# A decoder layer with rotary attention and a gated Hadamard FFN: queries and keys rotated feature-major and stored as score-ready rows, four attention units' maxima taken beside the FFN, division by the softmax sums moved to the output

## The reference, cut to what matters

```python
x  = L0_attn_X                                  # (4, 1024, 256)
xn = _layernorm(x)                              # over the 256 features
# attention, 16 heads of 16
Q, K, V = xn @ Wq.T, xn @ Wk.T, xn @ Wv.T
r0 = cos * x0 - sin * x1                        # x0, x1: even and odd features of a head
r1 = sin * x0 + cos * x1
scores  = einsum('bhqd,bhkd->bhqk', Qr, Kr) * 16 ** -0.5
scores  = where(causal, finfo.min, scores)
pattern = softmax(scores, axis=-1)
s = einsum('bhqk,bhkd->bqhd', pattern, V) @ Wo.T
# FFN
h = fwht(xn * SU_ug) / 64
h = silu(h @ W_gate.T * ws_gate * 64) * (h @ W_up.T * ws_up * 64)
g = silu(fwht(h * SU_dp) / 64 @ W_down.T * Wscale_dp * 64)
out = x + s * g
```

## Time and profile before

| what | before |
|---|---|
| median of 3 runs | 1056.6 us (1055.76 to 1058.85) |
| profiled execution, its own time | 1058.22 us |
| its span | 1056.5 us |
| TensorE (PE) busy | 944.7 us, 89% |
| VectorE (DVE) busy | 702.3 us, 66% |
| ScalarE (ACT) busy | 489.1 us, 46% |
| GpSimd (POOL) busy | 196.1 us, 19% |
| TensorE clock granted, mean | 0.962 of full |

### The profile page before, as it was taken

One profiled execution on the slowest core, in us unless ns is written; L12 is line 12 of the kernel. 1 busy time (PEld: TensorE's weight loads), 2 busy tenths in 40 slices (PEclk: granted clock), 3 DMA queues, 4 the chain that ended last, 5 costly groups with the idle time before them and its releaser, 6 DMA issues. The chain is left out here.

```text
span 1056.5 us, 17971 instructions
## 1 busy us (share of the span) xinstructions
PE 944.7 (89%) x6560; PEld 600.6 (57%) x6560; DVE 702.3 (66%) x1274; ACT 489.1 (46%) x729; POOL 196.1 (19%) x359
## 2 busy tenths in 40 slices
PE   5699999999999978889888888888888888888887
PEld 1488888888888865444444544444444444445355
DVE  6756465564655647677778778777877777787325
ACT  2332333333332320366565656656565665556641
POOL 4200000000000100122222222232222223221226
PEclk9899999999999995599999999999999999999989
DMA  5102112022030220011101201210210212012124
GB/s 177 41 1 100 67 33 99 0 99 93 6 129 14 86 83 37 5 73 42 63 19 42 76 11 37 82 37 7 81 37 14 74 42 76 7 41 87 51 70 180
DMA packets 46982, 61.19 MB, mean 58 GB/s; under 512 B 19008, under 2 KB 30272, under 8 KB 46912
## 3 DMA queue, kind: packets, MB, share of 16 engines
q1 hardware_dynamic: 45296, 57.11, 16.2%
q10 hardware_dynamic: 1616, 3.15, 1.0%
HBM read 34.81 MB, written 25.17 MB: 57 GB/s over the span
## 5 line engine op out<-in xcount | busy, mean ns | idle before, releaser
L926 DVE TENSOR_REDUCE maxes<-ps 128x1 f32<-128x512 f32 (+3 forms) x640 | 372.1, 632 | 75.1 <-PE ps L775 62.3
L885 ACT ACTIVATE probs<-ps 128x1024 f32<-128x1024 f32 (+3 forms) x384 | 296.7, 809 | 173.6 <-PE ps L796 169.8
L767 PE MATMUL ps<-k_t,q_t 64*128 64x512 f32 (+3 forms) x768 | 223.5, 406 | 51.1 <-DVE maxes L926 50.9
L767 PEld LDWEIGHTS ps<-k_t,q_t 64*128 64x128 f32 x768 | 116.6, 195 | 118.9 <-DVE maxes L926 108.2
L717 POOL TENSOR_SCALAR_AFFINE_SELECT probs<-probs 128x256 f32<-128x256 f32 x256 | 104.6, 409 | 398.5 <-ACT probs L885 396.1
L796 PE MATMUL ps<-q_t,k_t 64*128 64x512 f32 (+3 forms) x768 | 164.8, 418 | 3.5 <-ACT probs L885 2.2
L811 PE MATMUL ps<-probs,v_ones 128*32 128x512 f32 (+3 forms) x1536 | 165.7, 504 | 0.2 <-POOL probs L717 0.2
L796 PEld LDWEIGHTS ps<-q_t,k_t 64*128 64x128 f32 x768 | 77.1, 188 | 90.0 <-ACT probs L885 54.3
L242 PE MATMUL ps<-xh,wug_hi 128*128 128x512 f32 x256 | 101.4, 396 | 2.6 <-DVEq L336 2.6
L314 ACT ACTIVATE silu<-ps,scales 128x512 f32<-128x512 f32 x64 | 44.1, 689 | 126.9 <-PE ps L242 126.9
L367 DVE SCALAR_TENSOR_TENSOR hid<-ps,scales,silu 128x512 f32<-128x512 f32 x64 | 48.1, 751 | 82.1 <-ACT silu L314 82.1
(11 more groups left out here) (94 smaller groups left out, 1151.4 us busy)
## 6 DMA issues: line engine op xcount, KB each, us to landing
loaded<-scr_qkv SPq DMA_DIRECT2D x16, 768.0 KB, 4.3
scr_qkv<-qkv SPq DMA_DIRECT2D x8, 1152.0 KB, 4.4
x_sb<-in_x SPq DMA_DIRECT2D x10, 512.0 KB, 4.6
scr_gate<-y_sb SPq DMA_DIRECT2D x8, 512.0 KB, 3.9
gate_in<-scr_gate SPq DMA_DIRECT2D x8, 512.0 KB, 5.4
xt_in<-in_xt SPq DMA_DIRECT2D x8, 512.0 KB, 6.3
scr_heads<-o_nat SPq DMA_DIRECT2D x32, 128.0 KB, 2.3
out_t<-res SPq DMA_DIRECT2D x8, 512.0 KB, 2.7
```

Of the source, the lines that this page charges most:

```text
L767: last = pe.matmul(ps[:, bank, n * w:(n + 1) * w], q_t[par][rows, p, i * P:(i + 1) * P], k_t[par][rows, p, part * CH:part * CH + w], start ...
L885: act.activation(probs[:, (NS * par + s) % RING, p, :, 0:w], ps[:, bank:bank + 2, 0:w], ACT.Exp, scale=SCALE).then_inc(exp_ok, 1)
L926: dve.tensor_reduce(maxes[:, part, i, 2 * pairs[0] + e:2 * pairs[-1] + e + 1:2], ps[:, turns['m', k, e], 0:n * w].rearrange('p (h k) -> p ...
```

## The change

Projection block. The q and k projections are made feature-major (weights stationary, 512 tokens streaming; even and odd features of all heads in two banks), rotated by four wide VectorE products a chunk (turn) and added by GpSimd, split by ScalarE and GpSimd, and stored by SyncE in twelve transfers a chunk as rows that can be loaded as score operands (store_kinds): 48 rows for each head, high, high, low for queries and high, low, high for keys. hid_lo and the next chunk's normalisation move from VectorE to GpSimd. The chunk is 24 slots with a ring of four banks. From chunk 2 on, the 80 max tiles of units 2, 3, 0, 1 (in this order) and their 8 row transposes are spread over the slots, with two banks of their own. The loops over chunks are written out.

Attention block. No slots, to_rows, to_tokens, split_hi, split_lo or copies; operands come by DMA straight from scr['qk'], 48 of 64 rows of each half used (49 with the row of maxima). The 240 tiles of units 4 to 15 are spread over steps 3 to 174 of 192: 68 steps hold two, 104 one, 20 none. Each unit's rows are loaded twice, for the tiles (q_m, k_m) and for the scores (q_s, k_s). The undivided products go to HBM. A chain of steps (CHAIN) for each of 6 chunks then loads the sums, inverts them, writes the inverses to HBM, reads them back spread over the heads' rows, multiplies on GpSimd, and makes the output products among the steps (piece). Chunks 6 and 7 stay behind the last step. The output block is gone.

```diff
-        qk = self.loaded[:, :, 0:2 * HG * DH].rearrange('p t (h d) -> p t h d', d=DH)
-        eng.tensor_copy(self.slots[:, :, :, 0:DH], qk)
-        eng.tensor_copy(self.slots[:, :, 0:HG, DH:2 * DH], qk[:, :, 0:HG, :])
-        eng.tensor_copy(self.slots[:, :, HG:, 3 * DH:], qk[:, :, HG:, :]).then_inc(self.hi_ok, 1)
...
-    def split_lo(self, eng, v):
-        eng.wait_ge(self.hi_ok, v + 1)
-        qk = self.loaded[:, :, 0:2 * HG * DH].rearrange('p t (h d) -> p t h d', d=DH)
-        eng.tensor_tensor(self.slots[:, :, 0:HG, 3 * DH:], qk[:, :, 0:HG, :], self.slots[:, :, 0:HG, 0:DH].bitcast(F32), op=ALU.subtract)
-        eng.tensor_tensor(self.slots[:, :, HG:, DH:2 * DH], qk[:, :, HG:, :], self.slots[:, :, HG:, 0:DH].bitcast(F32), op=ALU.subtract).then_inc(self.lo_ok, 1)
...
-    PER_STEP = [0, 1, 2, 2, 2, 2, 2, 2, 2, 2, 2, 1]
-    FILLS = TB // 2
...
-            def to_rows(v, n):
-                f, of_k = (n // 2, n % 2)
-                bank = turns['t', n, 0]
-                wait_turn('t', n, 0, v)
-                if n == 0:
-                    pe.wait_ge(hi_ok, v + 1)
-                    pe.wait_ge(lo_ok, v + 1)
-                for p in range(NPAIR):
-                    for t in range(2):
-                        pair = slots[:, 2 * f + t, HG * of_k + 2 * p:HG * of_k + 2 * p + 2, :]
-                        last = pe.transpose(ps[:, bank, (2 * p + t) * P:(2 * p + t + 1) * P].bitcast(F32R), pair.rearrange('p a b -> p (a b)'), ident_r[:, :])
-                last.then_inc(t_ok, 1)
...
-            def to_tokens(u, c):
-                bank = turns['o', c, 0]
-                wait_turn('o', c, 0, u)
-                pe.wait_ge(o_read, QC * u + c + 1 + 1)
-                for t in range(TPC):
-                    last = pe.transpose(ps[:, bank, t * P:(t + 1) * P], o_raw[c][:, t * P:(t + 1) * P], ident[:, :])
-                last.then_inc(ot_ok, 1)
...
-                tiles = list(range(PIECE[s], PIECE[s + 1])) if nxt else []
-                if nxt and s < FILLS:
-                    to_rows(v, 2 * s)
-                    to_rows(v, 2 * s + 1)
-                if s == 1 and prev:
-                    weigh(u - 1, vpar, NS - 1)
...
-            def normalise(u, c):
-                dve.wait_ge(ot_ok, QC * u + c + 1)
-                rows = ps[:, turns['o', c, 0], :].rearrange('p (t h d) -> p t h d', t=TPC, d=2 * DH)
-                inv = o_inv[:, c]
-                dve.reciprocal(inv, rows[:, :, :, DH]).then_inc(inv_ok, 1)
-                dve.wait_ge(inv_ok, QC * u + c + 1)
-                dve.wait_ge(o_out[c], 16 * u + 16)
-                dve.tensor_tensor(o_nat[c][:, :, :].rearrange('p t (h d) -> p t h d', d=DH), rows[:, :, :, 0:DH], inv.rearrange('p t (h one) -> p t h one', one=1).to_broadcast([P, TPC, HG, DH]), op=ALU.mult).then_inc(o_ok, 1)
...
+EARLY_UNITS = (2, 3, 0, 1)
+NEARLY = len(EARLY_UNITS)
+turn_of = lambda v: EARLY_UNITS.index(v) if v < NEARLY else v
...
+def load_qk(eng, scr, q, k, v, done):
+    b, g = divmod(v, NG)
+    for which, dst in ((0, q), (1, k)):
+        for e in range(2):
+            src = scr['qk'][which, b, HG * g + e:HG * g + e + 3:2]
+            eng.dma_start(dst[SLOT * e:SLOT * e + ROWS, :, :].bitcast(F32), src.rearrange('x r t -> r x t')).then_inc(done, 16)
...
+            last = pe.matmul(ps[:, banks[e], n * w:(n + 1) * w], q[rows, p, i * P:(i + 1) * P],
+                             k[rows, p, part * CH:part * CH + w], start=True, stop=not masked)
...
+        NW = 24
+        G_AT = (0, 4, 7, 11, 15, 17, 19, 21)
+        U_AT = (1, 5, 8, 12, 16, 18, 20, 22)
+        Q_AT, K_AT, V_AT, X_AT = ((2, 3), (9, 10), (6, 23), (13, 14))
+        DOWN_AFTER = {8: 0, 10: 1, 12: 2, 16: 3, 18: 4, 20: 5}
+        bank_of = lambda n: n % 4
+        D_BANK, M_BANK = (4, 6)
...
+        uses = []
+        for n, v in enumerate(EARLY_UNITS):
+            for k in range(NT):
+                uses.append(('tile', v, k))
+                if k == 1 and n:
+                    uses.append(('rows', EARLY_UNITS[n - 1], 1))
+                if k == LOW_TILES + 1:
+                    uses.append(('rows', v, 0))
+        uses.append(('rows', EARLY_UNITS[-1], 1))
+        SPAN = NW * (NCHUNK - 2) - 4
+        use_at = {}
+        for n in range(len(uses)):
+            slot = n * SPAN // len(uses)
+            use_at.setdefault((2 + slot // NW, slot % NW), []).append(n)
+        tile_turn = lambda v, k: NT * turn_of(v) + k
...
+                for n, (low, odd) in enumerate(images):
+                    dst = scr['qk'][which, b, :, n * HALF:(n + 1) * HALF, half * CH:(half + 1) * CH]
+                    eng.dma_start(dst, kinds[which][:, 2 * low + odd, :].bitcast(F32)).then_inc(qk_out[which], 16)
+            def store_v(c, n):
+                eng.wait_ge(v_taken, 2 * c + n + 1)
...
+            def load_early(v):
+                par = v % 2
+                if v == EARLY_UNITS[0]:
+                    eng.wait_ge(sh.ones_set, 1)
+                if turn_of(v) < 2:
+                    for which in range(2):
+                        eng.wait_ge(qk_out[which], 2 * 6 * 16)
+                else:
+                    eng.wait_ge(et_ok, 2 * (tile_turn(EARLY_UNITS[turn_of(v) - 2], NT - 1) + 1))
+                load_qk(eng, scr, sh.q_s[par], sh.k_s[par], v, sh.qs_in[par])
...
+            store_gate(NCHUNK - 1)
+            load_rows(eng, sh, EARLY_UNITS[2], 1)
+            for half in range(QC):
+                load_rows(eng, sh, EARLY_UNITS[3], half)
...
+            def hidden_low(c, ib):
+                n = IB * c + ib
+                pool.wait_ge(hh_ok, n + 1)
+                pool.tensor_tensor(hid_lo[:, ib % NHB, :], hid[:, ib % 2, :], hid_hi[:, ib % NHB, :].bitcast(F32),
+                                   op=ALU.subtract).then_inc(hl_ok, 1)
+            def rotate(c, which):
+                pool.wait_ge(turned, 2 * c + which + 1)
+                pool.tensor_tensor(rot[:, 0, 0, :], rot[:, 0, 0, :], rot[:, 0, 1, :], op=ALU.subtract)
+                pool.tensor_tensor(rot[:, 1, 0, :], rot[:, 1, 0, :], rot[:, 1, 1, :], op=ALU.add).then_inc(rot_ok, 1)
+            def kinds_low(c, which):
+                pool.wait_ge(kind_hi_ok, 2 * c + which + 1)
+                pool.wait_ge(rot_ok, 2 * c + which + 1)
+                pool.tensor_tensor(kinds[which][:, 2:4, :], rot[:, :, 0, :], kinds[which][:, 0:2, :].bitcast(F32),
+                                   op=ALU.subtract).then_inc(kind_lo_ok, 1)
...
+                    for use in use_at.get((c, n), ()):
+                        early(use)
...
+            def turn(c, which):
+                bank = bank_of((Q_AT, K_AT)[which][0])
+                pos = slice(c % QC * CH, (c % QC + 1) * CH)
+                dve.wait_ge(qk_ok, 2 * c + which + 1)
+                if 2 * c + which:
+                    dve.wait_ge(kind_lo_ok, 2 * c + which)
+                dve.tensor_tensor(rot[:, 0], ps[:, bank:bank + 2, :], table[:, 0:2, pos], op=ALU.mult)
+                dve.tensor_tensor(rot[:, 1], ps[:, bank:bank + 2, :], table[:, 1:3, pos], op=ALU.mult).then_inc(turned, 1)
...
+    LATE = [(v, k) for v in range(NEARLY, NU) for k in range(NT)]
+    START, SPAN = (3, 172)
+    tile_step = lambda v, k: START + (NT * (v - NEARLY) + k) * SPAN // len(LATE)
...
+    chain_at = {NS * (NG * (b + 1) + c): QC * b + c for b in range(B - 1) for c in range(QC)}
+    chain_at[NS * (NU - 1) + 5] = QC * (B - 1)
+    CHAIN = {'load': 3, 'recip': 5, 'keep': 6, 'spread': 8, 'scale': 11, 'high': 12, 'low': 13,
+             ('piece', 0): 15, ('piece', 1): 18, ('sum', 0): 16, ('sum', 1): 19,
+             ('out', 0): 17, ('out', 1): 20}
+    chains = {}
...
+            def load_max(v):
+                if v >= NEARLY + 2:
+                    eng.wait_ge(tile_ok, 2 * NT * (v - NEARLY - 1))
+                load_qk(eng, scr, q_m[v % 2], k_m[v % 2], v, qm_in[v % 2])
...
+            def load_heads(ch):
+                b, c = divmod(ch, QC)
+                wait_heads(eng, NG * b + NG - 1, c)
+                heads = scr['heads'][ch].rearrange('g (h r) n -> g h r n', h=HG)
+                if ch:
+                    eng.wait_ge(inv_ok, ch)
+                    eng.wait_ge(scaled, ch)
+                src = heads[:, :, DH, :].rearrange('g h (k n) -> (g h) k n', n=SUMS)
+                eng.dma_start(sums[:, :], src).then_inc(sums_in, 16)
+                for o in range(DC):
+                    src = heads[NG // DC * o:NG // DC * (o + 1), :, 0:DH, :].rearrange('g h r n -> (g h) r n')
+                    eng.dma_start(o_in[:, o, :], src).then_inc(heads_in, 16)
+                if ch >= 2:
+                    eng.wait_ge(gated_ok, DC * (ch - 1))
+                    eng.wait_ge(res_ok, DC * (ch - 1))
+                eng.dma_start(gate_in[:, ch % 2], scr['gate'][ch].rearrange('o p n -> p o n')).then_inc(more_in[ch % 2], 16)
+                eng.dma_start(xt_in[:, ch % 2], xt_d[ch]).then_inc(more_in[ch % 2], 16)
+            def keep_inverse(ch):
```

(32 more changed lines are left out.)

1437 lines of the change are left out of this document (710 added, 727 removed).

## The result

| what | before | after |
|---|---|---|
| median | 1057.6 us (1055.4 to 1059.0, 16 runs) | 1043.1 us (1032.3 to 1054.3, 16 runs) |
| ratio | | 0.985, 95% interval 0.983 to 0.987 |
| profiled span | 1056.5 us | 1042.1 us |

The change is 1.5% faster; forecast were 952 us and a range of 892 to 1018. The sign was right, the size was not. New as well: the runs lie 22 us apart (15 without the slowest), those of before 3.6.

A forecast was written before the change was run, and what follows sets the result against it. TensorE bounds the FFN; in the units no engine is full and two-tile steps wait on PSUM banks. Weights 41.7, FFN 392.9, gap 11, units 465 and end 42 sum to 952 us, range 892 to 1018.

The forecast's parts named there:

- Weights, gap, end: Stages outside FFN and units: weights unchanged at 41.7 us, gap 11 (8 to 13), output end 42 (34 to 50).
- FFN, the old work: FFN's existing products and GpSimd's new operations: 0 us added, hidden, bounds 0 to 3 us a chunk.
- FFN, the early tiles: 80 max tiles moved into the FFN: 0.50 us each, 40, plus 2 transposes and 5 loads; FFN 393, 370 to 415.
- Filling: Filling of unit 0 before the units: gone, -38.7 us, since its maxima, rows and operands are there.
- Units, the tiles and steps: Attention steps without, with one, with two tiles: 1.67, 1.9, 2.8 us, 421 in all; cold clock 8 more.
- rival A: Units: the 0.63 us wait in each of 68 two-tile steps could vanish, 43 us, giving 909; chance 0.14.
- Rival C: 48-row pairs no longer run side by side: 0.17 us more for each of 768, 131 us, giving 1083; chance 0.05.
- Rival D: Units: one-tile steps keep TensorE at 1.2 GHz, up to 190 us more, 1060 or more; chance 0.04.
- Units, the chains: Six late-division chains among the steps: 2 us of waiting each, bounds 0 and 6, 12 in all; output products 18 more.
- Rival B: New chains late behind one SyncE queue: 6 us a chain (+24), GpSimd in FFN +24, giving 1000; chance 0.20.
- Transfers: Units' loads and stores: 76 MB in 465 us, 163 GB/s, hidden since 303 GB/s had been seen.

The follow-up runs named there:

- no_chains: The change with the late-division chains of chunks 0 to 5 left out, only chunks 6 and 7 done behind the last step: 957.4 us.
- one_queue: The change with a new step table, SyncE issuing the chain's small transfers ahead of operand loads, Wo first, early tiles from slot 10: 984.6 us.
- small_ahead_act: one_queue with operand loads near a chain moved behind its small transfers, and those small transfers issued on ScalarE's queue: 1024.1 us.
- early_small: The change with a new step table, ScalarE's queue issuing the chain's small transfers, Wo first, early tiles from slot 10: 1019.5 us.
- chain_late: The change with the same work, each link of the chains given more steps: 1015.0 us.

## Why the prediction was wrong, by its steps

**Weights, gap, end.** Forecast 41.7, 11 and 42; measured 44.6, 11.0 and 41.8. Right but for 2.9 us, which the sum had at 0: TensorE waits 10.5 us for the first normalised x where it waited 6.2 before; why it is later was not looked into.

**FFN, the old work: right.** Chunks 0 and 1, which have no tiles, take 41.2 and 43.3 us against 43.2 before. GpSimd's groups (busy us, mean ns, idle before) are near the estimates, 1.29 for 512 (1.2) and 2.39 for 1024, and the normalisation is 4 x 1.22 us and not 3; and TensorE's waits of that stage (us, times, longest) name hid_lo with 0.8 us in all:

```profile
L351 POOL TENSOR_TENSOR hid_lo<-hid,hid_hi 128x512 fp32r<-128x512 f32 x64 | 82.4, 1288 | 138.1 <-ACT hid_hi L507 138.1
L362 POOL TENSOR_TENSOR kinds<-rot,kinds 128x1024 fp32r<-128x1024 f32 x16 | 38.3, 2392 | 28.0 <-ACT kinds L520 28.0
L178 POOL TENSOR_SCALAR xn<-x_sb,moments,rstd 128x256 f32<-128x256 f32 x28 | 33.9, 1222 | 0.7
```
```profile
PE ps L107 <- DVE mx L588: 8.9, 12, 1.4
PE ps L107 <- DMA k_s<-scr_qk: 6.7, 1, 6.7
...
PE ps L433 <- POOL hid_lo L351: 0.8, 2, 0.7
```

**FFN, the early tiles: a term mis-sized.** The step "a change of the array's division costs 0.10, and a tile brings two: 0.50 each" failed. The row it came from had a change from products of 128 rows and 32 columns of the array to a pair of 64 rows and 128 columns; here it is between 48 rows and 128, with 128 columns in both, and a tile costs 0.43 + 0.10 + 0.11 = 0.64 where it is unmasked and 512 wide, 0.73 on the mean of chunks 3 to 6 (11.0 us a chunk for 15 tiles and row transposes). Over six chunks that is 66 us where 42 were forecast, 24 of the 27, VectorE's late reads (8.9, not forecast) among them. Chunk 2, with the first load, took 9.8 us more than the chunks after it where 5 were forecast: 6.7 for the load, and a clock of 0.93 around it. Chunk 0 took 2 less than before. The bound for a tile was 0.72, so this stage left its bounds, 370 to 415, by 5 us; the upper one was generous, since 80 x 0.72 and the 7 us beside it make 411.
The Trainium skill, TensorEngine Tiling (Array Packing), Key Properties, says that changing the tiling mode drains TensorE; the trace agrees in that a change in and out costs 0.41 us.

**Filling: right.** It is gone.

**Units, the tiles and steps: right.** 26.5 for 27.3 a unit, and 440.5 us without chains for 435 forecast (465 less 18 and 12). Unit 0 took 41.9 of them where some 25 and 8 for the cold clock were due: 12 in step 3, for Wo and the first tile's operands, were not in the sum. The other units made it up. Of rival A's 5 x 0.63 = 3.2 us a unit at most 0.8 is to be seen. Rival C did not happen: the two halves of a 48-row pair are done in 0.50 us together, as the row of L107 above shows. Rival D's sign came, 0.87, but not its mechanism: one-tile steps do not keep the clock down, as unit 1 ran at 1.00 and the longest stretches of half clock stand at the stalls.

**Units, the chains: here it failed.** The step is "the sums arrive for VectorE about when it asks, behind 2 MB of operand loads. 2 us a chain, bounds 0 and 6: 12." The chains cost 84 us with their 18 of products, 14 a chain. Rival B had the mechanism and 6 us a chain; it was given 0.20 and too little. Two things were missed.

First, **Transfers**: "448 to 454 shows 303 GB/s, so they are hidden". I asked whether the bytes fit into the time, and they do (a unit with share 0.92 loses nothing). For the sums I named the 2 MB ahead and gave it no price, and for the inverses and spread ones I did not ask what they find ahead of them. Also the rate was not to be had: 0.70 of the engines' time moved 143 GB/s, so they are full at 204, not at 303. 1.5 MB of operands is 7.4 us of all sixteen engines, 2 MB 10; by the straight line above 1.5 MB ahead make a landing of 8.5 us and 2 MB one of 11. Each link of a chain that stands behind one is late by that much, and a chain has three (sums, inverses, spread ones).

Second, the chain was costed at the engine that waits (ScalarE for GpSimd), not at the engine that issues. SyncE waits in its order for each landing, and the loads behind it come late and together with the next small transfer. And the long stalls are followed by stretches at 1.2 GHz, which the sum had once, at the start. The Trainium skill, TensorE: Matmul & The Clock Gate, on HAM oscillation, says that idle gaps bring the half clock back; the change's units agree, 0.87 against 0.95 without chains, and I had used the rule for the gap and the end alone. Unit 6 of no_chains, at half clock without an idle time over 0.24 us before it, does not fit it: idle gaps are not all that does it.

## What to carry to other kernels

A transfer's cost is what was issued before it. For each small transfer on which an engine waits, write down the bytes ahead of it on all queues, at the rate those transfers reach themselves, and put it ahead of the bulk loads; a queue of its own helps little if the bulk is issued first. A new table of steps and another order of issue, in one_queue, gave 985 us, 58 less than the change and 6.7% below the kernel before (0.930 to 0.936).

## What the runs showed of the hardware that was not expected

- A 32 KB transfer on ScalarE's queue took 11.1 us (inverses, small_ahead_act) and 13.6 (sums, early_small) behind bulk loads on SyncE's queue, 1.5 and 2.2 us in small_ahead_act without them. The queue gave it no priority.
- A 32 KB transfer took 1.7 us and some 4.6 more for each MB issued before it and not yet moved (256 transfers of 16 runs, either queue).
- Issuing can take long: one store of 256 KB, usually 0.34 us, took 7.75 us of SyncE in chain_late and 10.4 in early_small, with 2.7 and 2.9 MB issued and not yet moved.
- Loads of operands, 48 partitions in pieces of 4 KB, moved 167 GB/s with the 16 engines busy all the time (541 to 547 us of no_chains), where the wider loads of before made 303 at 0.88. Why, no run shows.
- 17 us at 1.2 GHz cost 7 us in a unit without a chain, with no idle time of TensorE over 0.24 us before the clock fell.
- A 48-row pair between 128-row products costs 0.41 us more than its columns.
